# SyncE fetches more of the gathered tiles row by row, and starts earlier

## What is computed

```python
h   = relu(layernorm(x))
W   = einsum('rb,bio->rio', comp, basis)          # one 64x64 matrix for each relation
msg = h[src] * weight
s   = segment_sum(msg, etype * N + dst)           # by relation and destination
y   = relu(einsum('rni,rio->no', s, W) + bias) + relu(h @ res_w.T + res_b)
out = x + (y - mean(y)) * rsqrt(var(y) + eps) * gamma + beta
```

## Time and profile before

| | |
|---|---|
| timed runs, median of 3 | 1977.18 us (1973.91 to 1977.34) |
| profiled execution, span | 2559.4 us |
| TensorE matmul busy | 1675.1 us (65%) |
| POOL busy | 1474.2 us (58%) |
| VectorE busy | 1040.2 us (41%) |
| ScalarE busy | 1003.6 us (39%) |
| moved by DMA | 308.66 MB, mean 121 GB/s |
| mean granted clock of TensorE | 0.690 of full speed |

### The profile page before, as it was taken

One profiled execution on the slowest core, in us unless ns is written; L12 is line 12 of the kernel. 1 busy time (PEld: TensorE's weight loads), 2 busy tenths in 40 slices (PEclk: granted clock), 3 DMA queues, 4 the chain that ended last, 5 costly groups with the idle time before them and its releaser, 6 DMA issues. The chain is left out here.

```text
span 2559.4 us, 29252 instructions
## 1 busy us (share of the span) xinstructions
PE 1675.1 (65%) x6522; PEld 817.4 (32%) x6571; DVE 1040.2 (41%) x3394; ACT 1003.6 (39%) x2898; POOL 1474.2 (58%) x1565
## 2 busy tenths in 40 slices
PE   1267677867787767466666677768778787872223
PEld 1222222323233222244444434434434343331112
DVE  0442013335233211255555535636546363632324
ACT  0255543424343332655555526526436252610001
POOL 7265535554465553366666666666666666666664
PEclk9997878878798878555555575575565757575656
DMA  7066667767687765111111111111111111111112
GB/s 141 24 244 264 263 250 275 304 234 285 254 341 300 291 230 198 45 42 40 43 40 40 43 28 41 42 27 39 40 31 39 31 40 31 35 23 41 39 41 63
DMA packets 120893, 308.66 MB, mean 121 GB/s; under 512 B 49361, under 2 KB 49644, under 8 KB 95395
## 3 DMA queue, kind: packets, MB, share of 16 engines
q1 hardware_dynamic: 56622, 233.21, 23.4%
q0 software_dynamic: 49504, 50.79, 10.6%
q10 hardware_dynamic: 14588, 22.76, 3.2%
HBM read 80.28 MB, written 226.35 MB: 120 GB/s over the span
## 5 line engine op out<-in xcount | busy, mean ns | idle before, releaser
L618 POOL DMA_INDIRECT shared<-z_table,idx_all x1019 | 967.3, 949 | 605.8 <-issue 233.6
L590 POOL DMA_INDIRECT acc<-in_x,idx_all x520 | 493.9, 950 | 448.5 <-DMA head_rows<-acc 299.7
L1238 PE MATMUL zps<-wp,res 128*128 128x512 bf16 x1915 | 503.3, 414 | 188.8 <-issue 79.9
L655 ACT ACTIVATE zst<-zps 128x512 f32<-128x512 f32 x480 | 276.9, 599 | 365.3 <-PE zps L1238 223.1
L762 ACT ACTIVATE res<-res,hw 128x64 f32<-128x64 f32 x1056 | 357.5, 426 | 104.2 <-issue 53.8
L1371 PE MATMUL mps<-wp,res 128*128 128x160 f32 (+4 forms) x528 | 271.9, 620 | 158.7 <-issue 84.4
L1238 PEld LDWEIGHTS zps<-wp,res 128*128 128x128 bf16 x1956 | 190.1, 103 | 490.6 <-issue 164.5
L1105 DVE TENSOR_SCALAR shared<-iota,rel_all,wgt_all 128x36 f32<-128x36 f32 (+9 forms) x1035 | 307.9, 326 | 62.0 <-ACT res L729 61.5
L1356 PE MATMUL zps<-shared 128*64 128x36 f32 (+9 forms) x1354 | 208.3, 317 | 146.2 <-issue 72.7
L749 ACT ACTIVATE res<-res,hm 128x64 f32<-128x64 f32 x528 | 176.0, 334 | 224.9 <-issue 132.2
L1356 PEld LDWEIGHTS zps<-shared 128*64 128x64 f32 x1354 | 143.7, 197 | 351.6 <-issue 283.3
(11 more groups left out here) (202 smaller groups left out, 1306.9 us busy)
## 6 DMA issues: line engine op xcount, KB each, us to landing
z_table<-zst SPq DMA_DIRECT2D x194, 1024.0 KB
wp<-z_table SPq DMA_DIRECT2D x1792, 0.2 KB
head_rows<-acc SPq DMA_DIRECT2D x66, 256.0 KB
res<-head_rows ACTq DMA_DIRECT2D x64, 256.0 KB
shared<-z_table,idx_all POOLq DMA_INDIRECT x1019
acc<-in_x,idx_all POOLq DMA_INDIRECT x520
wp<-z_table ACTq DMA_DIRECT2D x256, 0.2 KB
zst<-in_x ACTq DMA_DIRECT2D x12, 256.0 KB
```

Source lines behind the costliest of these rows:

```text
L590: e.indirect_dma_start(out=ring[:, b % NRING, i, :], out_offset=None, in_=x, in_offset=bass.IndirectOffsetOnAxis(ap=idx_first[:, t:t + 1] ...
L618: e.indirect_dma_start(out=ys[:, q % NY, :], out_offset=None, in_=table[:, :], in_offset=bass.IndirectOffsetOnAxis(ap=idx_all[:, col:col + ...
L655: e.activation(to, frm, ACT.Copy).then_inc(s_ez, 1)
L1238: last = e.matmul(to, lhsT=stationary(px, pw), rhs=moving(px, pw), start=(a == 0), stop=(a == 2))
```

## The change

Two constants of the loop that fills `owner` change. `SP_FIRST` goes from 150 to 48 and `SP_EVERY` from 64 to 36: SyncE gets its first tile when POOL's count has reached 48, and another for each 36 on. `NSP` and everything else stays. SyncE's tiles become 27 (47, 87, 127, 159, 199, 239, 271, 311, 343, ... 943, 975, 1023), ScalarE's stay the same two, and POOL keeps 1006. What is computed is the same.

```diff
 REGS = 32
 ACT_TILES, ACT_EVERY, ACT_LATE = 2, 80, 15
-SP_EVERY, SP_FIRST, NSP = 64, 150, 3
+SP_EVERY, SP_FIRST, NSP = 36, 48, 3
 X_STEP = 16
```

## The result

The changed kernel takes 2100.16 us (median of 4, 2097.9 to 2102.34) against 1975.98 us for the kernel before: ratio 1.0625, 95% interval 1.061 to 1.064. The forecast was 2095 us, with the bound moving from POOL to SyncE's issuing of rows.

The account below looks back on a forecast made before the run. POOL's back-to-back gathers bound the kernel before, SyncE's row issuing the changed one: first TensorE tile 721, SyncE's start 2.6, 27 tiles 1337, about 7 and 20.2 to the end make 2088; 7 for ScalarE gives 2095 us, range 1960 to 2350.

Parts of the forecast that it names:

- POOL gathering back to back from start to end: On POOL before the change: a gather each 1.25 us without other standstill bounds the timed runs, 1979 against 1977.18 us measured.
- Mostly added by the recording: In the earlier profile: the span's excess of 582 us over the timed median comes mostly from profiling, not from timed runs.
- a span of 3560 to 3750 us: New profile's length on the earlier profile's clock, with SyncE's tile at 92 to 98.9 us; the earlier span was 2559.4.
- ScalarE's rows beside it: Last stretch, where ScalarE fetches its two tiles beside SyncE: SyncE's rows get dearer, 0 to 72 us, put down as 7.
- the 13.2 us wait: POOL standing still after its 36-slot ring fills, as table gathers begin 57 us before TensorE can take the first tile.
- the sum for the kernel before (1979 us): POOL's time: first gather at 4.3, 1546 steps of 1.25, 29.5 us after the last gather, plus 13.2 us standing still.
- The undisturbed stretch of the earlier trace: SyncE's 31 rows in 9.87 us, from which a row was priced at 0.322 us and a tile at 49.5.
- The point of break-even, 44.4 us a tile: SyncE's tile price at which 27 tiles take the 1200 us POOL needs to let TensorE reach tile 1023.
- the band of 46 to 54 us: Price of a SyncE tile in the main case, SyncE as the bound: 2000 to 2210 us, chance 0.58.
- SyncE keeping up: Rival at SyncE's row issue: below 44.4 us a tile POOL stays the bound, 1961 us; chance 0.13.
- Dearer rows: Rival on SyncE: rows cost more than undisturbed, from stalls or contention with ScalarE; 2376 us at 60 a tile; chance 0.22.
- The cap of 84 us: Upper limit of a SyncE tile's price: 14 tiles took at most 1182 us in the timed runs; gives some 3020 us.

Follow-up runs that it names:

- the second one-load kernel: Changed kernel, but each tile's registers are loaded once, kept and used four times, without a second MOVE per row (output not the reference's): 1960.73 us, ratio 0.992.
- the cadence of 40: Changed kernel with SP_EVERY 40 in place of 36, still from the 48th gather, so 24 SyncE tiles: 1964.98 us, ratio 0.9937; in noisy series 1.171 and 1.170.
- the kernel with the second MOVE: Changed kernel with one register load per tile in place of four, but a second MOVE for each row (output not the reference's): 2148.77 us, ratio 1.087; noisy 1.311.
- the kernel that starts at 150: Changed kernel with SP_FIRST 150 in place of 48, SP_EVERY still 36, so 24 SyncE tiles: 2978.36 us, ratio 1.166, run in the noisy condition only.

## Why the prediction was right, and where it wasn't

**What bounds the kernel before.** "POOL gathering back to back from start to end" holds as far as the runs reach: with SyncE fast enough (the second one-load kernel, and the cadence of 40) the time is POOL's steps, and it falls by 1.25 us for each gather taken away, 16.4 us for 13 and 11.6 for 10. A quiet trace of the kernel before itself is missing.

**"Mostly added by the recording" is wrong.** Timed runs of the kernel before took 2554 and 2560 us in two series. The stretched trace shows a condition of the machine, whose cause stays open. The argument still worked for the changed kernel, since I took only undisturbed steps from that trace and held their sum against the timed median, and those medians were quiet. The same mistake produced the one forecast that failed outright, a span of 3560 to 3750 us in the new profile: it is 2100.5. In the noisy condition the changed kernel itself was not run.

**The terms of the sum**, forecast against the new trace:

| term | forecast, us | measured, us |
|---|---|---|
| first table gather on POOL (inside the next term) | 664 | 675.0 |
| first tile on TensorE | 721 | 694.0 |
| from there to SyncE's first row or load | 2.6 | 0.5 (its load) |
| a SyncE tile | 49.5 | 51.1 |
| 27 of them | 1337 | 1381 |
| from SyncE's last row to the end | 27 | 25 |
| ScalarE's rows beside it | 7 | some 2, in the 1381 |
| span | 2095 | 2100.5 |

Two errors of opposite sign largely cancel: the first tile 27 us too late, the 27 tiles 44 us too short. That the total is only 5 us off is luck; that SyncE is the bound, and its price within 4%, is not. The 57 us between the first table gather and TensorE's first tile came from the noisy trace, where work of phase one was late; undisturbed it is 19 us, POOL's ring is never full at that point, and the 13.2 us wait of the earlier trace rows that I added to reach 1979 doesn't exist. That the sum for the kernel before (1979 us) met the median so closely was luck too. By the quiet traces the 13.2 us are too much, and so are some 6 of the 29.5 us behind the last gather (23.3 in the second one-load kernel, 1958.7 - 1935.4). Too little are the 528 x 1.25 us of the first phase, by 11 us (the head gathers take 956 ns on average, and the table is waited for 4.6 us), and the 1.25 of a step, which is 1.255 on average, 5 us in all. The 11 us and the 5 us are from the traces of other kernels, for the kernel before has no quiet one.

The tile was 1.6 us too cheap, which is 44 us for 27. In the changed kernel a row without a load costs 0.322 us at the median, as forecast, but 0.330 on average, since some 330 of the 3456 rows take longer, up to 0.67 us. That is 1.0 of the 1.6 us. A stretch of that trace has 160 rows with four loads between them; it is made of 155 steps of 0.332 us on average and four of 2.49.

```profile
696.51 61.65 SPq L444 DMA_DIRECT2D wp<-z_table  x160
```

The other 0.6 us are the loads, at 2.22 us more than a row's step where I took 2.07. The undisturbed stretch of the earlier trace rows was read rightly, and the quiet traces have one of the same length; to take it for the average was the slip.

```profile
712.81 9.87 SPq L445 DMA_DIRECT2D wp<-z_table  x31
```

(This is from the second one-load kernel. The earlier trace rows has 31 rows in the same 9.87 us.) Three SyncE tiles were issued beside ScalarE's rows; they took 51.6 to 52.0 us each, which is some 2 us in all where 7 were put down.

**The bound moves, and which wait takes over.** Both as written: waits of TensorE on SyncE's slots before 25 of 27 tiles, POOL's idle time growing on matmuls of 1356, 1006 gathers, no price for three slots. The point of break-even, 44.4 us a tile, was met from the other side: at 44.4 us POOL is the bound again. The price measured, 51.1 us, lies in the band of 46 to 54 us that had the chance of 0.58.

**The rule of the pages.** The estimate of 0.43 us a row from the Trainium skill ("DMA: Bandwidth & Descriptors", table of sequencer time, with the clock of "Advanced Engine Details and Errata") would have given 2440 us; the trace disagrees, at 0.322 with the MOVE. The Trainium skill's rule that sequencer time is usually small beside the DMA ("DMA: Bandwidth & Descriptors", section "Issuing engines are not separate DMA queues") is turned round here: the time on the sequencer set the end of the kernel, and the kernel with the second MOVE moved that end by changing it alone.

**The rivals.** SyncE keeping up was the right second: it is what happens 6.7 us a tile lower. Dearer rows are what the noisy condition shows, 79 us a tile on average. The cap of 84 us was drawn from quiet runs and doesn't hold there: three tiles of the kernel that starts at 150 take 103 us each.

## What to carry to other kernels

When one queue hands out work to another, compare two rates, not two busy shares: what the helper needs for one piece, all its instructions counted, and what the main engine needs for the pieces between. Here 27 tiles cost 124 us, and 24 tiles gained 12. Beyond the crossing the end is the helper's start plus the number of its pieces times their price; below it each piece is worth only what it takes off the main engine, here 1.25 us, against a tile that comes 6 us late (51.1 against 45). Price small DMAs by the issuing sequencer's instructions, MOVEs and register loads among them, not by bytes, and take the average step and not the undisturbed one.

## What the runs showed of the hardware

- Row DMAs of 256 bytes from SyncE, one MOVE and one issue each: 0.322 us at the median and 0.330 on average; one more MOVE of 34 ns costs 66 ns a row with its gap ((52.9 - 44.4) / 128); 32 registers loaded from SBUF: 2.18 us of recorded work, and 2.54 us from the issue before the load to the issue after it.
- TensorE waited 187.5 us for SyncE's tiles in the kernel with 24 of them, and its POOL lost nothing measurable, with single waits up to 30.8 us. In the changed kernel POOL first stands still when no wait has yet been longer than 19.6 us. So the length of a single wait doesn't decide. What does is whether TensorE falls further behind POOL with each tile, by some 6 us in the changed kernel, until the 36 slots (45 us of POOL's work) are used up. Idle time of TensorE is no measure of the loss.
- The same kernel took 1976 us in four series and 2554 and 2560 us in two, and on chip 3 it did both. In the noisy ones the longest MOVE of SyncE's rows is 802 to 1422 ns, by trace, where it is 38 ns otherwise, and while the table is made DMAs move some 225 to 345 GB/s against 376 to 406. Both noisy series had four kernels and the quiet ones a single kernel of mine; six series are too few to call that the cause, and it was not pursued.
